# A decoder layer on one NeuronCore: another order of the tasks on all five engines

## What is computed

```
xk, xv, xr = x * mix + shifted(x) * (1 - mix)
k, v, r    = xk @ Wk.T, xv @ Wv.T, xr @ Wr.T
rwkv       = sigmoid(r) * wkv(decay, first, k, v)        # a recurrence along the tokens
x1         = layernorm(x + rwkv @ Wo.T)
q          = rope(rms_norm(x1 @ Wq.T)); kk = rope(rms_norm(ctx @ Wk.T)); vv = ctx @ Wv.T
x2         = layernorm(x1 + softmax(q kk.T / 4) vv @ Wo.T)
gate, up   = silu(bitlinear(x2, w_gate)), bitlinear(x2, w_up)     # 1024 wide
out        = layernorm(x2 + bitlinear(gate * up, w_down))
```

## Time and profile before

| | us |
|---|---|
| median of three runs | 1313.85 (1309.25 to 1318.02) |
| span of the profiled execution (the page gives no other time of its own for it) | 1322.8 |
| PE, matmuls busy | 1157.0 (87%) |
| DVE busy | 1083.4 (82%) |
| ACT busy | 868.5 (66%) |
| POOL busy | 579.1 (44%) |

### The profile page before, as it was taken

The page is one execution under the profiler, slowest core; times in us unless marked ns, Lnnn a source line. Parts: engine busy times, 40 slices in busy tenths (PEclk is TensorE's granted clock), DMA queues, the critical chain, the costliest instruction groups (busy, mean ns, idle before and its releaser), DMA issues. The chain is left out here.

```text
span 1322.8 us, 22903 instructions
## 1 busy us (share of the span) xinstructions
PE 1157.0 (87%) x6434; PEld 889.3 (67%) x6466; DVE 1083.4 (82%) x2447; ACT 868.5 (66%) x1581; POOL 579.1 (44%) x1142
## 2 busy tenths in 40 slices
PE   1547999999999999989999999989999999998784
PEld 1436777777777777767777777767777777776551
DVE  3678898988888999888888898888888898886333
ACT  0434667877677777777677666766776667776444
POOL 4244455444445455543445455444444455444200
PEclk6877899988888989988888899988888899898775
DMA  6000001111100111110100111111101111100000
GB/s 198 16 21 3 21 23 29 29 29 29 29 20 15 31 30 29 30 29 29 29 26 8 31 30 29 29 29 29 29 4 30 31 29 29 28 14 11 11 9 17
DMA packets 83117, 37.07 MB, mean 28 GB/s; under 512 B 54837, under 2 KB 82485, under 8 KB 82997
## 3 DMA queue, kind: packets, MB, share of 16 engines
q1 hardware_dynamic: 82997, 35.56, 10.1%
HBM read 24.62 MB, written 8.39 MB: 25 GB/s over the span
## 5 line engine op out<-in xcount | busy, mean ns | idle before, releaser
L499 POOL TENSOR_TENSOR mneg<-zeros,mv 128x2 f32<-128x2 f32 x96 | 18.7, 195 | 445.3 <-DVE mv L1076 445.3
L895 PE MATMUL pb<-q_t,k_blk 128*128 128x256 f32 (+1 forms) x640 | 181.0, 386 | 1.9 <-ACT p_t L692 1.5
L906 PEld LDWEIGHTS pb<-v_blk,p_t 128*128 128x128 f32 (+1 forms) x1280 | 160.3, 208 | 16.2 <-ACT p_t L692 10.8
L906 PE MATMUL pb<-v_blk,p_t 128*128 128x34 f32 (+2 forms) x1280 | 163.9, 292 | 7.1 <-ACT p_t L692 7.1
L666 ACT ACTIVATE gate_silu<-pg,gate_scale 128x512 f32<-128x512 f32 x128 | 88.1, 689 | 103.6 <-PE pu L941 103.6
L697 ACT ACTIVATE hid_int<-hid,magic_p,hid_scale 128x1024 f32<-128x1024 f32 x64 | 78.9, 1236 | 103.4 <-DVE hid_scale L1230 103.4
L1268 DVE TENSOR_REDUCE m_pad<-pb 128x4 bf16<-128x308 f32 x256 | 113.5, 465 | 19.6 <-PE pb L876 19.6
L895 PEld LDWEIGHTS pb<-q_t,k_blk 128*128 128x128 f32 (+1 forms) x640 | 98.7, 188 | 43.7 <-ACT p_t L692 8.3
L1084 DVE SCALAR_TENSOR_TENSOR mix<-dx,vec,x_t 128x256 f32<-128x256 f32 x192 | 117.9, 666 | 6.9 <-POOL dx L562 6.9
L692 ACT ACTIVATE p_t<-pb 128x512 f32<-128x512 f32 (+1 forms) x160 | 95.0, 595 | 40.9 <-PE pb L896 40.0
L711 ACT ACTIVATE x<-raw,nmean,rstd 128x256 f32<-128x256 f32 x128 | 69.9, 593 | 55.5 <-POOL nmean L507 55.0
(11 more groups left out here) (174 smaller groups left out, 3056.0 us busy)
## 6 DMA issues: line engine op xcount, KB each, us to landing
x_t<-xt SPq DMA_DIRECT2D x32, 256.0 KB, 2.8
x_tok<-x SPq DMA_DIRECT2D x32, 256.0 KB, 3.2
out<-outb SPq DMA_DIRECT2D x32, 256.0 KB, 3.2
ctx_t<-ctxt SPq DMA_DIRECT2D x32, 77.0 KB, 3.0
w_sb<-wts SPq DMA_DIRECT2D x8, 256.0 KB, 4.5
v_blk<-v_sb SPq DMA_DIRECT2D x128, 9.6 KB
hid<-wg SPq DMA_DIRECT2D x1, 1024.0 KB, 7.3
hid_int<-wu SPq DMA_DIRECT2D x1, 1024.0 KB, 9.5
```

What stands on the lines that cost most here:

```text
L895: mm(dst, k_blk[p][:, g, cols], q_t[p][:, g, :], start=True, stop=False)
L906: last = mm(pb[j][:, c0:c0 + NHEAD[n] * VW], p_t[0:k, q, s, j * P:(j + 1) * P], v_blk[p][0:k, g, n, 0:NHEAD[n] * VW], start=q == 0 and s == 0,
```

## The change

Five lists are written in another order; no instruction inside a task is changed, added or removed. The tasks that cross the end of a list get another lag (`s[3]` at the top is `s[2]` at the bottom), which is the same place in the cycle. PE's list no longer reaches further than `s[4]`, so its depth is 4. SP's list is as it was.

```diff
 # POOL
-                if s[3]: q_rope(s[3][0])
                 if s[3]: q_mean(s[3][0])
-                if s[2]: rwkv_den(s[2][0])
-                if s[3]: k_mean(s[3][0])
                 if s[3]: k_rope(s[3][0])
                 if s[3]: q_newton(s[3][0])
+                if s[3]: k_mean(s[3][0])
+                if s[2]: rwkv_num(s[2][0])
                 if s[3]: k_newton(s[3][0])
-                if s[2]: rwkv_num(s[2][0])
                 if s[3]: k_scale(s[3][0])
                 if s[4]: ln_scale(1, s[4][0])
                 if s[2]: ln_scale(0, s[2][0])
+                if s[1]: rwkv_den(s[1][0])
                 if s[0]: rwkv_dx(*s[0])
                 if s[5]: ln_scale(2, s[5][0])
+                if s[2]: q_rope(s[2][0])
 # PE
...
+                if s[3]: attend(s[3][0], s[3][1], s[3][2], 1, 0)
+                if s[3]: attend(s[3][0], s[3][1], s[3][2], 1, 1)
                 if s[3]: attend(s[3][0], s[3][1], s[3][2], 0, 0)
+                if s[3]: attend(s[3][0], s[3][1], s[3][2], 1, 2)
                 if s[3]: attend(s[3][0], s[3][1], s[3][2], 0, 1)
                 if s[3]: attend(s[3][0], s[3][1], s[3][2], 0, 2)
+                if s[2]: q_transpose(s[2][0])
                 if s[3]: attend(s[3][0], s[3][1], s[3][2], 0, 3)
...
-                if s[2]: q_transpose(s[2][0])
                 if s[4]: hidden_transpose(s[4][0], 0)
+                if s[2]: keys_transpose(s[2][0])
                 if s[3]: attention_transpose(s[3][0])
-                if s[2]: keys_transpose(s[2][0])
                 if s[4]: hidden_transpose(s[4][0], 1)
...
+                if s[2]: score(s[2][0], s[2][1], 0)
                 if s[1]: rwkv_out(s[1][0], 1)
-                if s[2]: score(s[2][0], s[2][1], 0)
+                if s[2]: score(s[2][0], s[2][1], 1)
+                if s[0]: rwkv_in(s[0][0], 1, 0)
+                if s[2]: score(s[2][0], s[2][1], 2)
                 if s[4]: down(s[4][0], 0)
...
```

ACT's list, around the transposes:

```diff
+                if s[1]: reciprocal(s[1][0])
                 if s[2]: power_k(s[2][0])
-                if s[1]: reciprocal(s[1][0])
                 if s[4]: hidden_scaled(s[4][0], 0)
+                if s[4]: hidden_scaled(s[4][0], 1)
                 if s[2]: q_transposed(s[2][0], s[2][1])
-                if s[4]: hidden_scaled(s[4][0], 1)
+                if s[4]: hidden_integers(s[4][0], 0)
                 if s[3]: attention_transposed(s[3][0])
                 if s[2]: keys_blocked(s[2][0], s[2][1])
+                if s[0]: weight(s[0][0], 0)
+                if s[5]: ffn_apply(*s[5])
                 if s[0]: weight(s[0][0], 1)
```

More of the change, by code:

```diff
@@ L991, in body @@
                 if s[1]: rwkv_out(s[1][0], 0)
+                if s[2]: score(s[2][0], s[2][1], 0)
                 if s[1]: rwkv_out(s[1][0], 1)
-                if s[2]: score(s[2][0], s[2][1], 0)
+                if s[2]: score(s[2][0], s[2][1], 1)
+                if s[0]: rwkv_in(s[0][0], 1, 0)
+                if s[2]: score(s[2][0], s[2][1], 2)
                 if s[4]: down(s[4][0], 0)
-                if s[2]: score(s[2][0], s[2][1], 1)
-                if s[2]: score(s[2][0], s[2][1], 2)
-                if s[0]: rwkv_in(s[0][0], 1, 0)
                 if s[0]: rwkv_in(s[0][0], 1, 1)
+                if s[2]: score(s[2][0], s[2][1], 3)
                 if s[0]: rwkv_in(s[0][0], 2, 0)
@@ L1009, in body @@
                 if s[2]: score(s[2][0], s[2][1], 5)
+                if s[2]: score(s[2][0], s[2][1], 6)
                 if s[1]: queries(s[1][0], 1)
-                if s[2]: score(s[2][0], s[2][1], 6)
                 if s[2]: score(s[2][0], s[2][1], 7)
@@ L1286, in body @@
             def body(s):
-                if s[3]: k_squares(s[3][0])
-                if s[3]: q_squares(s[3][0])
-                if s[2]: rwkv_state_v(s[2][0])
-                if s[5]: ffn_gate(s[5][0], 3)
-                if s[5]: ffn_hidden_max(s[5][0], 1)
-                if s[2]: rwkv_den2(s[2][0])
-                if s[5]: ffn_scale(s[5][0], 0)
-                if s[2]: rwkv_current(s[2][0])
-                if s[5]: ffn_scale(s[5][0], 1)
-                if s[1]: rwkv_mix(s[1][0], s[1][1], 1)
-                if s[1]: rwkv_mix(s[1][0], s[1][1], 2)
+                if s[5]: ffn_hidden_max(s[5][0], 1)
+                if s[1]: rwkv_mix(s[1][0], s[1][1], 1)
+                if s[3]: q_scaled(s[3][0])
+                if s[1]: rwkv_mix(s[1][0], s[1][1], 2)
+                if s[5]: ffn_scale(s[5][0], 0)
+                if s[2]: rwkv_den2(s[2][0])
+                if s[5]: ffn_scale(s[5][0], 1)
+                if s[5]: ffn_scale(s[5][0], 2)
+                if s[2]: rwkv_state_v(s[2][0])
+                if s[5]: ffn_scale(s[5][0], 3)
                 if s[1]: rwkv_max(s[1][0])
                 if s[1]: rwkv_z(s[1][0])
-                if s[5]: ffn_scale(s[5][0], 2)
-                if s[2]: rwkv_newton(s[2][0], 0)
-                if s[5]: ffn_scale(s[5][0], 3)
-                if s[3]: q_scaled(s[3][0])
-                if s[2]: rwkv_newton(s[2][0], 1)
                 if s[4]: normalise(s[4][0], 0)
                 if s[4]: normalise(s[4][0], 1)
+                if s[2]: rwkv_newton(s[2][0], 0)
+                if s[1]: rwkv_exponent(s[1][0], 2)
+                if s[2]: rwkv_newton(s[2][0], 1)
+                if s[1]: rwkv_exponent(s[1][0], 1)
                 if s[2]: rwkv_newton(s[2][0], 2)
                 if s[1]: rwkv_exponent(s[1][0], 0)
-                if s[1]: rwkv_exponent(s[1][0], 1)
-                if s[1]: rwkv_exponent(s[1][0], 2)
                 if s[4]: attention_residual(s[4][0], s[4][1])
@@ L1327, in body @@
                 if s[5]: ffn_residual(s[5][0], 1, s[5][1])
-                if s[1]: rwkv_state_1(s[1][0])
                 if s[3]: maxima(s[3][0], 2)
                 if s[5]: ln_stats(2, s[5][0])
+                if s[1]: rwkv_state_1(s[1][0])
                 if s[4]: ffn_gate(s[4][0], 0)
-                if s[5]: ln_aggregate(2, s[5][0])
                 if s[3]: maxima(s[3][0], 3)
                 if s[3]: maxima(s[3][0], 4)
+                if s[5]: ln_aggregate(2, s[5][0])
+                if s[1]: rwkv_v(s[1][0])
                 if s[3]: maxima(s[3][0], 5)
                 if s[4]: ffn_gate(s[4][0], 1)
+                if s[3]: maxima(s[3][0], 6)
                 if s[4]: ffn_hidden_max(s[4][0], 0)
-                if s[3]: maxima(s[3][0], 6)
                 if s[3]: maxima(s[3][0], 7)
                 if s[4]: ffn_gate(s[4][0], 2)
-                if s[1]: rwkv_v(s[1][0])
                 if s[0]: rwkv_mix(s[0][0], s[0][1], 0)
+                if s[2]: k_squares(s[2][0])
+                if s[2]: q_squares(s[2][0])
+                if s[4]: ffn_gate(s[4][0], 3)
+                if s[1]: rwkv_current(s[1][0])
             schedule(dve, body, 5, warm)
```

19 lines of the change are left out of this document (6 added, 13 removed).

## The result

The changed kernel took 1230.61 us (median of four executions, 1225.34 to 1233.32), the kernel before 1312.76 beside it: a ratio of 0.936, 95% interval 0.9323 to 0.9397. The profiled execution took 1232.12 us, with a span of 1230.3. The forecast was 1274; 1228 was rival 1. Now and then an execution shows a lower granted clock throughout and takes some per cent longer; such executions are left out of the ratios, and the profiled one of the run pe_old was such (1346.71 us at a clock of 0.79).

The account below looks back on a forecast made before the run. A loop through PE and DVE was taken to bound the kernel, its period depending on PE's clock. Periods of 36.7 and 35.2, half each, gave 36.0: 31 × (37.28 − 36.0) = 40 us off 1313.85, so 1274 us, range 1226 to 1320.

Parts of the forecast that it names:

- rival 1: PE's half-clock stretch vanishes with its idle time; PE's period 33.7, DVE binds at some 34.5, 1228 us; chance 0.20.
- PE's wait for `qr`, −1.06: On PE at the attend block: `qr` made earlier on DVE removes the whole wait, 1.06 us a period.
- New waits of PE, +0.3: On PE: near ties for `kr`, `o_t`, raw and hid add 0.3 us a period, bounds 0 to 1.2.
- The clock, −0.5 a period: PE's half-clock stretch: long (period 36.7) in one period of two, short (35.2) in the other, so 36.0.
- rival 3: Low clock reaches PE's attend products; with 20 of 40 in it the period is 38.75, the time 1359 us; chance 0.11.
- DVE's Newton steps, −1.63 beside the wait: On DVE: newton_t and rec_neg move into its wait for the output product, shortening DVE's loop by 1.63 to 35.65 us.
- Contention, −0.5 (from +1.0 to −1.5): GpSimd beside VectorE: fewer held-up vector operations, −0.5 us a period for DVE, worth nothing while PE binds.
- The other moves, 0: Reordering on ACT, exponents in reverse, rwkv_current last and PE's depth 4 cost nothing; ACT busy 26.7, POOL 17.7 of 37.5.
- The loop's turn: PE's wait at the hardware loop's turn, 0.38 us a period, given no term of its own.

Follow-up runs that it names:

- pe_old: The changed kernel with PE's list of the kernel before, the other engines' lists new: 1251.08 us, ratio 0.9508.
- qs_early_only: The kernel before with only `qr` made early on DVE, behind the third mix: 1323.06 us, ratio 1.006.
- qt_back: The changed kernel with `q_transpose` moved back behind all 40 attend instructions on PE: 1259.42 us, ratio 0.9552.
- before_fill: The kernel before with six dense products of 512 columns, results unread, added ahead of `q_transpose` on PE: 1310.47 us, ratio 0.9922.
- pool_old: The changed kernel with GpSimd's (POOL's) list of the kernel before: 1258.98 us, ratio 0.9483.
- newton_back: The changed kernel with two Newton steps put back ahead of `o_n` on DVE: 1264.25 us, ratio 0.9618.
- in_block: qt_back with one dense product, `rwkv_in(0, 1)`, moved from ahead of the attend products to the middle of them: 1283.52 us, ratio 0.9762.

## Why the prediction was right and wrong

- **PE's wait for `qr`, −1.06: right.** It is gone; in the ordinary period of the earlier trace rows it was 1.5 of the 2.18 idle. But the early `qr` alone doesn't do it (qs_early_only); the prediction named the queue behind it, `hid_int` and `o_n`, only as cases for new waits.
- **New waits of PE, +0.3: right in kind, too small.** The near ties add up to 1.0 in the ordinary period (`o_t`, `x`, `x_int`, `hid`), where two of 0.2 stood before, so +0.6. That PE's idle time fell by 1.08, as much as the mean wait for `qr`, is chance: 1.5 went and 0.6 came.
- **The clock, −0.5 a period: this step failed.** I took one period in two with the long stretch and one with the short, a period of 36.0. Measured: no stretch in an ordinary period, 2.78 us less PE time, as rival 1 had it with its 33.7 for PE (measured 33.62). The reason I gave, "nothing thins out the block", took the transpose inside it for nothing: `q_transpose` splits the 40 instructions in 24 and 16, and making them whole again costs 0.019 of the ratio, some 25 us, and 72 us of half-clock time. The forecast also took the drop to come behind the block, in the wait; rival 3 has it as its argument against. In the kernel before 8 of 23 drops come inside the block. Rival 1's condition, that idle time keeps the clock down, is not what the runs show either: without any wait there, qt_back still has 81.9 us at half clock.
The Trainium skill, "TensorE: Matmul & The Clock Gate", section "HAM oscillation — how this bites in real kernels", puts the lower clock down to PE standing idle. The runs agree in part: before_fill has 101 us less half-clock time than the kernel before, but qt_back has 81.9 with no wait above 0.5 us in the stretch.
- **DVE's Newton steps, −1.63 beside the wait: right in direction and place.** Without it the ordinary period is 1.0 longer, by the path through `o_n`. Missed: among the other new lists, Newton steps ahead of `o_n` would also hold up GpSimd's `knt` and `krs`.
- **Contention, −0.5 (from +1.0 to −1.5): mis-sized.** DVE's busy time in a period fell by 1.54, the good end. Some of the collisions were indeed removed and not moved, since the GpSimd work now falls beside reads of PSUM: `newton_t` is at 0.68, no mix at 1.49. With POOL's old list (pool_old) `newton_t` is at 0.68 too, so this did not come from POOL's list.
The Trainium skill, "SBUF — State Buffer", section "Who interferes with whom", has a VectorE instruction with two SBUF inputs and a GpSimd one that reads SBUF exclude each other. newton_back agrees, 0.22 against 0.77 and 0.65; my use of it, that collisions can only be moved, did not hold.
- **The other moves, 0: wrong.** ACT's and POOL's lists are worth some 20 and 16 us, because they set when `qrs` and `kr` come. Busy time (26.7 and 17.7 of 37.5) was no cover: ACT was idle for over a quarter and POOL for half of the time, and both were still late.
- **The loop's turn: left out.** I kept its 0.38 a period, PE's wait. That wait is 0.5 now (11.6 in 23 periods), and the turns cost 0.65 in all, since DVE waits too; another 0.29 are the last three periods. This is why the mean period is 34.56 and not 33.62. That rival 1's 34.5 came out is luck: its own working had DVE binding, with 0.5 for scores and some tenths for the turn, and what stands there instead is PE at 33.6 and nearly 1 for turns and drain.

The sum as measured, from 37.28: −2.78 for the clock and −1.08 for idle time in the ordinary period, +1.14 since the mean stands 0.94 above the ordinary period now and stood 0.20 below the long one of the earlier trace rows before: −2.72, times 31 is 84 us, and 8 more for fill and drain, which I had taken as they were.

What stays open: which property of the broken block lets the clock stay up. Breaking the block and leaving PE no idle time each remove part of the half-clock time; the one kernel that was to tell the block's density apart (in_block) changed the work ahead of it too. Also open is why every second loop turn, and not each, is followed by a half-clock stretch.

## What to carry to other kernels

Price a low-clock stretch as a case of its own and in full, not by half: where small products and a wait stand together, reordering can remove all of it or leave it, and that was the largest term here. Look, too, where in the stream the clock falls, and not only where it is low: here it fell among the small products, before the wait that I had looked at. Before taking a wait away, list what the same engine needs in the next 2 us, since the next one is waited for instead; and look at the chains through lightly used engines by when their results arrive, not by their busy share.

## What the hardware showed that I had not expected

- The clock fell to half inside a run of 40 small matrix products while PE had no idle time at all: 600.30 to 602.72 us in the kernel before, busy 2.42 of 2.42 us at 0.50.
- A vector instruction holds up a GpSimd instruction as well as the other way: 77x16 operations at 0.77 and 0.65 us beside `newton_t` and `rec_neg`, 0.22 beside the reads of PSUM.
- The clock of a kernel can rise and its time hardly move: before_fill ran at 0.97 instead of 0.91 in the middle and was 0.8% faster.
- In the changed kernel a turn of the hardware loop makes PE wait 2.3 us on average and costs 2.9 to 3.2 us, or 4.5 to 4.8 with the half-clock stretch behind it; three turns fewer gave about 1% of the time.
